# Last steps of an attention pipeline: group 15's rows, logits, choice and block tables placed ahead of shared expert work; one GpSimd scatter in two halves

## The reference, cut to what matters

```
x = x + 0.5 * ffn(layernorm(x))
x = x + attention(layernorm(x))      # causal linear attention, 16 heads of 8, feature map elu + 1
x = x + 0.5 * ffn(layernorm(x))      # the same weights as the first

ffn(x):
    logits = x @ gate_w                       # 8 experts
    top_v, top_i = top_k(logits, 2); top_p = softmax(top_v)
    routed = sum over the two chosen experts of top_p * (silu(x @ Wg[e]) * (x @ Wu[e])) @ Wd[e]
    shared = (silu(x @ Sg) * (x @ Su)) @ Sd   # hidden width 176
    return routed + shared
```

## Time and profile before

| | |
|---|---|
| median of 3 runs | 1202.69 us (1200.29 to 1203.06) |
| profiled execution | 1201.17 us, its span 1199.4 us |
| busy share of the span | PE 83%, PEld 62%, DVE 77%, ACT 52%, POOL 68% |
| mean granted TensorE clock | 0.947 |

### The profile page before, as it was taken

One profiled execution on the slowest core, in us unless ns is written; L12 is line 12 of the kernel. 1 busy time (PEld: TensorE's weight loads), 2 busy tenths in 40 slices (PEclk: granted clock), 3 DMA queues, 4 the chain that ended last, 5 costly groups with the idle time before them and its releaser, 6 DMA issues.

```text
span 1199.4 us, 31719 instructions
## 1 busy us (share of the span) xinstructions
PE 993.6 (83%) x9014; PEld 745.9 (62%) x9015; DVE 928.6 (77%) x2483; ACT 624.2 (52%) x1322; POOL 814.1 (68%) x855
## 2 busy tenths in 40 slices
PE   2656675999999977788888888888875799999993
PEld 1334444888999963455555555555542689898983
DVE  6787783678888865788888888888875467888885
ACT  5556561555555553455555555555523255555552
POOL 4677774677777776456667766667764377777774
PEclk9799896999999998999999999999986799999997
DMA  9411113243334310000000000000001324444452
GB/s 280 117 50 49 50 51 93 75 114 114 116 114 125 118 61 18 1 8 21 22 22 18 18 18 18 18 18 18 23 32 47 79 78 122 147 138 131 128 146 75
DMA packets 68613, 86.67 MB, mean 72 GB/s; under 512 B 13004, under 2 KB 56209, under 8 KB 68558
## 3 DMA queue, kind: packets, MB, share of 16 engines
q1 hardware_dynamic: 51278, 52.15, 15.7%
q0 software_dynamic: 17280, 33.87, 8.5%
HBM read 44.74 MB, written 43.04 MB: 73 GB/s over the span
## 4 chain that ended last, share of the span: by engine, by line
PE 26%; POOL 23%; issue 21%; DVE 14%; DVEq 6%; ACT 5%; DMA 2%; POOLq 1%; SPq 0%; ACTq 0%
POOL expert_results L547 16%; PE PSUM L1010 8%; POOL carrier L545 6%; PE PSUM L1012 5%; PE PSUM L873 3%; PE PSUM L875 3%; PE PSUM L874 3%; DVEq L1449 2%; PE PSUM L1128 2%; DVE which L1281 2%; POOL routed_rows L536 1%; DVEq L1301 1%; DVE shT L1218 1%; DVE X L1318 1%; DVE prod L1447 1%
## 5 line engine op out<-in xcount | busy, mean ns | idle before, releaser
L547 POOL DMA_INDIRECT expert_results<-ey,eidx x284 | 288.4, 1015 | 71.5 <-issue 70.6
L536 POOL DMA_INDIRECT routed_rows<-row,idx x256 | 252.8, 987 | 74.4 <-issue 70.6
L873 PE MATMUL PSUM<-eT,WGU 128*128 128x256 f16 x852 | 233.9, 275 | 1.6 <-issue 0.4
L874 PE MATMUL PSUM<-eT,WGU 128*128 128x256 f16 x852 | 233.7, 274 | 0.0
L875 PE MATMUL PSUM<-eT,WGU 128*128 128x256 f16 x852 | 233.7, 274 | 0.0
L732 ACT ACTIVATE esil<-PSUM 128x768 f32<-128x768 f32 x142 | 115.1, 810 | 226.0 <-PE PSUM L875 210.9
L561 POOL TENSOR_TENSOR space<-qk,val 128x1152 f32<-128x1152 f32 x64 | 138.3, 2171 | 92.4 <-DVE qk L1440 65.0
L1218 DVE SCALAR_TENSOR_TENSOR ehT<-eh,ehT 128x768 f16<-128x768 f32 x142 | 136.6, 962 | 70.4 <-ACT ehT L737 68.5
L873 PE MATMUL PSUM<-WD,ehT 128*128 x852 | 160.9, 220 | 7.6 <-DVE ehT L1218 3.9
L1010 PE MATMUL PSUM<-space,upto 128*128 128x320 f32 (+1 forms) x384 | 151.4, 504 | 12.6 <-DVE prod L1447 8.4
L874 PE MATMUL PSUM<-WD,ehT 128*128 x852 | 159.1, 220 | 0.0
(11 more groups left out here) (214 smaller groups left out, 2284.3 us busy)
## 6 DMA issues: line engine op xcount, KB each, us to landing
xe<-routed_rows SPq DMA_DIRECT2D x142, 130.0 KB
space<-expert_results SPq DMA_DIRECT2D x32, 512.0 KB, 3.7
expert_results<-ey,eidx POOLq DMA_INDIRECT x284
X<-in_L_attn_x_dram SPq DMA_DIRECT2D x16, 256.0 KB, 4.6
routed_rows<-row,idx POOLq DMA_INDIRECT x256, 2.3
out_dram<-X SPq DMA_DIRECT2D x16, 256.0 KB
routed_rows<-pad_rows SPq DMA_DIRECT2D x24, 130.0 KB
space<-in_L_ffn_Wg_dram SPq DMA_DIRECT2D x1, 1408.0 KB, 8.9
```

What stands on the lines that cost most here:

```text
L536: pool.indirect_dma_start(routed, bass.IndirectOffsetOnAxis(ap=idx[u][:, k, j:j + 1], axis=0), row[u][:, j, :], None).then_inc(s_scattered ...
L547: pool.indirect_dma_start(result, bass.IndirectOffsetOnAxis(ap=eidx[u][:, h:h + 1], axis=0), ey[u][:, h, :], None, bounds_check=K * T - 1, ...
L873: pe.matmul(dst, a[0], b[0], start=start, stop=False)
L874: pe.matmul(dst, a[0], b[1], start=False, stop=False)
```

## The change

In steps 14, 15 and 16 alone the order of work is another; nothing is added to what is computed. The loop's steps are the same as before.

- TensorE: `project` is split into `project_tokens` (bias and residual) and `project` (the twelve matmuls); in step 14 `positions(30)` stands between the two. In step 15 `logits(31)` stands ahead of `down(30)`. `tables` is split into `fresh_sums` and `block_sums`; in step 16 `fresh_sums(1)` stands between the halves of `gate_up(31)`, `block_sums(1)` behind the second.
- VectorE: in step 15 `place(30)` is first, ahead of the wait for attention's last residual, and `choose(31)` stands ahead of `shared_add(30)`. In step 16 `place(31)`, `ends` and the first part of `tables` are first, then `shared(31, 0)`, `tables_sums`, `shared(31, 1)`, `tables_rows`.
- GpSimd: in step 15 the four scatters of the first choice of group 14 stand ahead of `row_low(31)`, the four of the second behind it.

```diff
--- before.py
+++ after.py
@@ -527,11 +527,12 @@
                           allow_small_or_imprecise_dtypes=True)
             pool.drain().then_inc(s_constants, 1)
 
-            def scatter(n, u):
-                pool.wait_ge(s_placed_rows, n + 1)
-                pool.wait_ge(s_row_words, n + 1)
-                pool.tensor_tensor(ticket[:, u:u + 1], ones32[:, 0:1], ones32[:, 0:1], ALU.mult).then_inc(s_ticket, 1)
-                for k in range(K):
+            def scatter(n, u, ks=range(K)):
+                if 0 in ks:
+                    pool.wait_ge(s_placed_rows, n + 1)
+                    pool.wait_ge(s_row_words, n + 1)
+                    pool.tensor_tensor(ticket[:, u:u + 1], ones32[:, 0:1], ones32[:, 0:1], ALU.mult).then_inc(s_ticket, 1)
+                for k in ks:
                     for j in range(NJ):
                         pool.indirect_dma_start(routed, bass.IndirectOffsetOnAxis(ap=idx[u][:, k, j:j + 1], axis=0),
                                                 row[u][:, j, :], None).then_inc(s_scattered[u], 16)
@@ -589,6 +590,9 @@
                             low(m + 2, xa[:, 1, :, :], 1, xa[:, 0, :, :], s_attn_high, s_attn_low)
                         if attend:
                             outer(m + 1, 1, 1)
+                        split = isinstance(m, int) and m == NG - 1
+                        if split:
+                            scatter(m + (NG - 1), 1 - u, range(1))
                         if route:
                             row_low(m + NG, u)
                         if ready:
@@ -597,7 +601,7 @@
                         for g in rest_of(m):
                             combine(g)
                         if settle:
-                            scatter(m + (NG - 1), 1 - u)
+                            scatter(m + (NG - 1), 1 - u, range(1, K) if split else range(K))
                     for q in range(2):
                         pool.memset(val[:, q, :, :, HD:VD], 1.0)
                     pool.drain()
@@ -943,7 +947,7 @@
                                    stop=(d == NJ), skip_group_check=True)
                 mm.then_inc(s_positions, 1)
 
-            def tables(f):
+            def fresh_sums(f):
 
                 pe.wait_ge(s_fresh, f + 1)
                 pe.transpose(PT[:, 0:P], fresh[:, :], ident[:, :])
@@ -953,6 +957,9 @@
                 pe.matmul(SUM_ALL, turned[:, 0:P], ones16[:, 0:1], start=True, stop=True)
                 pe.matmul(SUM_UPTO, before[:, :], turned[:, 0:1], start=True, stop=False)
                 pe.matmul(SUM_UPTO, ident[:, :], turned[:, 0:1], start=False, stop=True).then_inc(s_fresh_sums, 1)
+
+            def block_sums(f):
+
                 pe.wait_ge(s_offsets, f + 1)
                 pe.transpose(PT[:, 2 * P:3 * P], offset_step[:, :], ident[:, :]).then_inc(s_offsets_turned, 1)
                 pe.matmul(SUM_EXPERT, turned[:, P:2 * P], past[:, :], start=True, stop=True)
@@ -1022,7 +1029,7 @@
                     mm = pe.transpose(PT32[:, j * P:(j + 1) * P], y32[:, j, :], ident32[:, :])
                 mm.then_inc(s_y_turned, 1)
 
-            def project(m):
+            def project_tokens(m):
                 if not isinstance(m, int) or m > 1:
                     pe.wait_ge(s_shared_added, m + (NG - 1))
                 else:
@@ -1031,6 +1038,8 @@
                           start=True, stop=False)
 
                 pe.matmul(POS[1], ident_y[:, :], X[:, cols(m, GT)], start=False, stop=False)
+
+            def project(m):
                 pe.wait_ge(s_yaT, m + 1)
                 for j in range(NJ):
                     t = slice(j * P, (j + 1) * P)
@@ -1144,7 +1153,8 @@
                 if edge and n == 1:
                     pe.wait_ge(s_weights_low, 2)
                 if edge and n == NG - 1:
-                    tables(0)
+                    fresh_sums(0)
+                    block_sums(0)
                 if not edge or n > 0:
                     down(n - 1)
                 if not edge or 0 < n < NG - 1:
@@ -1160,6 +1170,8 @@
                         pe.wait_ge(s_qkv_parts, (m + 1) * 2 + 2)
                         pe.wait_ge(s_features, (m + 1) * 2 + 2)
                     gate_up(n - 1, 1 - u, 0)
+                    if isinstance(m, int) and m == NG:
+                        fresh_sums(1)
                 if attend:
                     running_sums(m + 1, 0, 1)
                     keep_warm(9)
@@ -1179,7 +1191,9 @@
                     for a in range(2):
                         qkv_products(m + 2, 1, a)
                 if isinstance(m, int) and m == NG:
-                    tables(1)
+                    block_sums(1)
+                if isinstance(m, int) and m == NG - 1:
+                    logits(n, u, (m + 1) * NJ)
                 if settle:
                     if isinstance(m, int) and m == NG:
                         pe.wait_ge(s_shared_added, n - 1)
@@ -1188,13 +1202,18 @@
                         down(n - 1, m)
                 if ready:
                     running_sums(m + 2, 0, 0)
-                if route:
-                    logits(n, u, (m + 2) * NJ if attend else (m + 1) * NJ)
+                if route and attend:
+                    logits(n, u, (m + 2) * NJ)
                 if attend:
                     y_transposes(m + 1, route)
+                ahead = isinstance(m, int) and m == NG - 2
+                if attend:
+                    project_tokens(m + 1)
+                if ahead:
+                    positions(n)
                 if attend:
                     project(m + 1)
-                if route:
+                if route and not ahead:
                     positions(n, (m + 2) * NJ + 1 if ready else 0)
 
             ffn[0] = 0
@@ -1334,6 +1353,9 @@
                 dve.tensor_copy(nb[:, :], nbi[:, :])
                 dve.drain()
                 dve.tensor_tensor(fresh[:, :], nb[:, E:(NG + 1) * E], nb[:, 0:NG * E], ALU.subtract).then_inc(s_fresh, 1)
+
+            def tables_sums(f):
+
                 dve.wait_ge(s_fresh_turned, f + 1)
                 dve.tensor_copy(turned[:, :], PT[:, 0:2 * P]).then_inc(s_fresh_T, 1)
                 dve.wait_ge(s_fresh_sums, f + 1)
@@ -1343,6 +1365,9 @@
                 dve.drain()
                 dve.tensor_scalar(past[:, :], block_no[:, :], last_block[:, 0:1], None, ALU.is_ge)
                 dve.tensor_tensor(offset_step[:, :], offset[:, 1:NG * E + 1], offset[:, 0:NG * E], ALU.subtract).then_inc(s_offsets, 1)
+
+            def tables_rows(f):
+
                 dve.wait_ge(s_offsets_turned, f + 1)
                 dve.tensor_copy(offset_turned[:, :], PT[:, 2 * P:3 * P]).then_inc(s_offsets_T, 1)
                 dve.wait_ge(s_block_sums, f + 1)
@@ -1505,6 +1530,8 @@
                 if edge and n == NG - 1:
                     ends()
                     tables(0)
+                    tables_sums(0)
+                    tables_rows(0)
                 shared(n, 0)
                 shared(n, 1)
                 if edge and n == 0:
@@ -1561,7 +1588,20 @@
 
             def streams(m, u, route, attending, ready, settle):
                 n = m + NG
-                end = isinstance(m, int) and m == NG
+                if isinstance(m, int) and m == NG:
+                    place(n - 1, 1 - u, m - 1)
+                    ends()
+                    tables(1)
+                    shared(n - 1, 0)
+                    tables_sums(1)
+                    shared(n - 1, 1)
+                    tables_rows(1)
+                    shared_low(n - 1)
+                    shared_add(n - 1, m - 1)
+                    return
+                last = isinstance(m, int) and m == NG - 1
+                if last:
+                    place(n - 1, 1 - u, m - 1)
                 if route:
                     dve.wait_ge(s_attention_added, m + 1)
                     moments(0, m)
@@ -1576,13 +1616,11 @@
                 if settle:
                     if attending:
                         dve.wait_ge(s_running_sums, (m + 1) * NJ + 3)
-                    place(n - 1, 1 - u, m - 1)
+                    if not last:
+                        place(n - 1, 1 - u, m - 1)
                 if attending:
                     attend(m + 1, 1, 0)
                 if settle:
-                    if end:
-                        ends()
-                        tables(1)
                     shared_low(n - 1)
                 if ready:
                     features(m + 2, 0)
@@ -1596,9 +1634,11 @@
                     features(m + 2, 1)
                 if attending:
                     divide(m + 1)
+                if last:
+                    choose(n, u, m)
                 if settle:
                     shared_add(n - 1, m - 1)
-                if route:
+                if route and not last:
                     choose(n, u, m)
                 if attending:
                     y_low(m + 1)
```

## The result

The changed kernel took 1198.8 us, median of 14 runs (1194.76 to 1201.48), against 1202.74 us for the kernel before (14 runs): ratio 0.9969, interval 0.9959 to 0.9978. So it is faster, by 3.9 us where 7.7 were forecast (1202.69 to 1195.0). Two more comparisons of the same two kernels gave 0.9962 (0.9949 to 0.9975) and 0.9966 (0.9945 to 0.9987); the three together say about 4.1 us, 0.3% of the time. Four single runs of 1730 to 5542 us (one each of e4, e11 and e15, one of the kernel before beside e16) are left out of the ratios. The changed kernel's profiled execution has a span of 1197.6 us.

The account below looks back on a forecast made before the run. TensorE bounds the expert stage; the pipeline's end is bound by waits hanging on `place(31)`. Starting it 7.25 us earlier takes the profiled 1201.17 to 1193.9, or 1195.4 from the median; forecast 1195.0 us, range 1191.0 to 1199.3.

Parts of the forecast that it names:

- What bounds: TensorE bounds the expert stage; at the pipeline's end engines wait for one another, all hanging on `place(31)`.
- Step 14, place(30) first: `positions(30)` runs in TensorE's wait from 900.5, `place(30)` in VectorE's 2.28 us gap, both at 0 cost.
- The scatter in halves: GpSimd, step 15: four scatters end at 909.0, `row_low(31)` keeps 909.54; margin 0.2 us, possible slip 0.5 taken as 0.
- Logits and choice first: Step 15: logits at 912.9, `chosen` at 915.4, `down(30)` delayed to about 913.2, `place(31)` starting at 916.6.
- Step 16: `place(31)` starts at 916.6 in place of 923.85, 7.25 us earlier; first load at 929.75, landed at 931.9.
- 12.31 us carried for SyncE: SyncE's time from the end of `place(31)` to the first load's issue, for ends, pads, numbers and load, assumed unchanged.
- Scatters beside choose(31): Step 15: GpSimd's scatters could hold up VectorE's `choose(31)` by a shared port lock, 0.96 us each; taken as nothing.
- The expert stage moves along: Expert stage moves as a whole, as long as before at 260.2 us, clock rising 4.2 us after its start.
- The clock: Claim that from 910 us TensorE runs at the lower level, 1.2 of 2.4 GHz.
- first rival: Less gain, another wait becomes the last: halved scatter, tables or `transposes(31)`; 3.5 to 5 us gained, 1197.5; chance 0.16.
- rival "less": Another wait at the pipeline's end becomes the last, leaving 3.5 to 5 us of gain, 1197.5 us; chance 0.16.
- first candidate: GpSimd's halved scatter in step 15: a longer gap in the first half makes `row_low` and all behind slip 0.5 us.

Follow-up runs that it names:

- e4: Changed kernel with steps 14 and 15 in the old order, scatters whole, and step 16 as changed; ratio to the kernel before 0.9974.
- e11: Changed kernel with the low rows of group 15 on VectorE and group 14's eight scatters whole and early; ratio to the kernel before 0.9933 (1193.1 us).
- e15: Changed kernel a third time, no edit, against the kernel before; ratio 0.9966.
- e16: Changed kernel with two more indirect DMAs on GpSimd behind group 13's scatters and a wait for their landing behind step 16; ratio to the kernel before 0.9954.
- e3: Changed kernel with step 16's `gate_up`, shared products, place, ends and tables in the old order, step 15 as changed; ratio to the kernel before 0.9993.
- e2: Changed kernel with group 14's eight scatters whole again, behind the low rows of group 15; ratio to the kernel before 0.9982.
- e14: Kernel before once more, no edit, for a further profile; ratio to itself 0.9996.
- e5: Kernel before once more, no edit, on a chip where all took longer; ratio to itself 0.9969, not used.
- e9: Changed kernel with eight one-column memsets at the start of GpSimd's step 14; run once for the profile, no ratio.
- e13: Changed kernel with one more GpSimd instruction at the start of step 15, some 5 us ahead of the scatters; ratio to the kernel before 0.9958.
- e10: Changed kernel with fourteen idle matmuls in TensorE's step 16, five ahead of `down` of group 15 and nine behind; ratio to the kernel before 0.9949.

## Why the prediction was right and wrong

- *What bounds*: right. The time hung on `place(31)`, and bringing it forward brought the first block forward (e3 and e4 take it apart).
- *Step 14, place(30) first*: right, in the gap, `pk` at 0.22, nothing to pay; no run isolates this part.
- *The scatter in halves*: this step failed. "`row_low(31)` can follow at 909.3 and its input is there at 909.46, so it keeps its 909.54" rested on a margin of 0.2 us and on a longer gap priced at 0.5 and then taken as 0. The gap had stood in the rows, 1.01 us at 913.48, where nothing waited for the next scatter; in its new place it is 2.22 us and delays the low rows by 1.73 and `place(31)` by 1.75 (e16 against the changed kernel). The prediction took the wait for a fixed length of 1.01; fixed was its end, 4.0 us after ScalarE lets GpSimd go on. It named `row_low(31)` after 910.5 (M + 7.2) as a sign of being wrong, and that came: M + 7.95. The halves are still worth 2.9 us of the stretch (e2).
- *Logits and choice first*: right once the low rows are in time. `place(31)` was forecast at M + 13.28; e2 and e16 have 13.18, the changed kernel 14.93.
- *Step 16*: right and a little better. From the end of the indices to the first block it was 13.9 us in the three profiles where 14.47 were carried over; before itself it was 13.84 in e14. The 12.31 us carried for SyncE held a way over pads and block numbers that ended later than the scatters in that one profile; that pads or scatters "need not be known" left these 0.5 us out. The tables were ready at 929.49, 4.4 us ahead of the load.
- *Scatters beside choose(31)*: none held it up, as was taken. Logits' sum to `chosen` took 2.06 us beside scatters (918.10 to 920.16).
- *The expert stage moves along*: not settled. The clock rose 5.9 to 6.3 us after the first block in the changed kernel, 4.2 and 4.6 in the kernel before; its stage is 261.0 on average against 260.2. That these 0.8 us come of the change is not shown: the kernel before rose after 6.8 us in e5, e9 with TensorE's order of the changed kernel after 3.6, and e3 and e13 rose after 6.3 us with stages of 260.2 and 260.3. Among themselves the changed kernel's three stages differ by 1.2.
- *The clock*: "from 910 us TensorE runs at the lower level" read one window for the whole stretch. In that profile the level was the upper one from 923.1 to 926.5, before it fell for the last time.
- *The range*: its upper end, 1199.3, is 1.8 us above the first rival's 1197.5, and not the 2.8 that the text names as the spread.

The account from profiles: stretch and expert stage together 296.1 and 295.0 us before, 291.3, 290.1 and 290.6 after; a gain of 4.9 between the means. Timed it is 4.1, with half an interval of 1.1, 1.6 and 2.5 us. Against the first profile, of the forecast 7.25, 1.65 is missing at `place(31)` (GpSimd's gap of 1.75, less 0.1 by which the rest was better), 0.5 was gained from the indices to the first block (14.47 to 13.96), which makes the 6.1 of the stretch, and 0.8 went in the expert stage, which makes 5.3; e14, where the stretch of the kernel before is 0.9 shorter, takes the mean down to 4.9. The 0.8 us between 4.9 and 4.1 lie within the intervals and within what the steps ahead of M vary by, and aren't settled. The rival "less" came true, by its first candidate, at over three times the price set on it; that it had 0.16 was too little for a margin of 0.2 us on an engine whose gaps were known to vary.

## What to carry to other kernels

Where a moved step is to fit ahead of another with a margin smaller than the longest gap that its engine shows, price the slip with that gap, not with the typical one, and check what is queued behind; GpSimd's longest in the profile of the kernel before was 2.38 us, ahead of a scatter of the first expert stage at 404.54. A reordering pays when it is made on all engines that meet at the end: the early place of group 15 needed GpSimd free of group 14, and each half alone brought less. Here an operation on a full engine that another could do in its idle time (the low rows, e11) was better moved than squeezed.

## What the runs showed of the hardware

GpSimd's indirect DMAs start 1.26 us apart, but at three of the 540 a wait of 1.0 to 2.4 us comes ahead, always at the same ones. At the one in the pipeline it is 2.21 or 2.22 us in the changed kernel and in the seven other kernels whose scatters of group 14 start right behind `words`, and it ends 4.0 us after ScalarE's instruction that ends GpSimd's idling; two more indirect DMAs ahead made it vanish, memsets did not. Most steps of the pipeline take 27.0 or 27.9 us, one or two 29.1 to 29.5: from the residual of group 0 to that of group 15 two profiles of one kernel differ by 3.9 us. TensorE's granted clock goes up and down within the last steps: in the changed kernel's first profile it fell 4.3 us ahead of the first block and rose 5.9 us after it, and in e10, with fourteen idle matmuls in gaps of 2.2 and 3.1 us, it stayed at the upper level.
